# Graph attention layer on one core: one-hots in rows at a pitch of 130, own rows and tails joined from other places, marks and reciprocals in PSUM

## The chip, the core and the metric

The kernel runs on one core of a Trainium2 chip. The time is that of the device for one execution, in microseconds, and comparisons are made by medians of such executions. TensorE (PE; PEld are its weight loads), VectorE (DVE), ScalarE (ACT), GpSimd (POOL) and SyncE (SP) work side by side and meet at semaphores. GpSimd, SyncE and ScalarE also issue DMAs.

## What is computed

12500 nodes of 32 features and 400000 edges sorted by destination. Each node is normalised and projected by the matrix of its type; each edge gets a score from source, destination, edge type and attributes; the scores of a node's incoming edges go through a softmax, and the messages are summed with these weights.

```python
h = jnp.maximum(_layernorm(x, axis=-1), 0.0)
xl = jnp.einsum('ni,nio->no', h, hetero_w[node_type]) + hetero_b[node_type]
ete = _lrelu(edge_type_emb[edge_type]); eae = _lrelu(edge_attr @ edge_attr_w)
alpha = _lrelu(jnp.concatenate([xl[dst], xl[src], ete, eae], axis=-1) @ att_w)
alpha = jnp.exp(alpha - segment_max(alpha, dst)[dst])
alpha = alpha / (segment_sum(alpha, dst)[dst] + 1e-16)
msg = jnp.concatenate([xl[src], eae], axis=-1) @ lin_w * alpha
out = x + segment_sum(msg, dst)
```

## The kernel before

Each of 128 partitions has 3125 successive edges, worked on in 125 chunks of T = 25 edges a partition. Chunks go through U = 5 sets of buffers; a hardware loop runs 24 times over five chunks, and the last five stand behind it. A prologue builds a table of 12544 rows of 34 numbers (projected features and the two partial scores), stores it, splits the destinations into five digits, and sorts out constants.

In the loop a chunk needs three things. First, the table rows of its 25 sources. 22 of them come by an indirect DMA each, issued by GpSimd (`gather_chunk`, L494). GpSimd runs up to two chunks ahead (AHEAD = 2), and five turns within a chunk wait for what VectorE did for the chunk two earlier (picks, sums). The other 3 (TS) are computed: `select` (L697) multiplies one-hots of the source (7 groups of nodes, a 128 x 128 one-hot each) with the table in three bf16 parts, 21 matmuls of 462 columns; `take_product` (L1058) masks the result and `take_sum` (L1064) reduces it into `gath`. VectorE writes these one-hots in two pieces: tile 0 of a chunk in `select_first` (seven writes of 128, L1037), tiles 1 and 2 in `select_others` (seven of 256), into one set of buffers, so each piece waits for the matmuls that read the last one. Second, the destination scores: `dst_onehot` (L1084) writes a one-hot of 122 x 3200 from five loaded digits, `dst_scores` (L711) multiplies it with the scores, and `picks` (L1071) takes the maximum over 128 columns, in seven pieces. Third, messages from the edge attributes (L720, L742).

VectorE goes through these in a written order: picks 0 and 1, attribute activation, one-hots of tiles 1 and 2 of the next chunk, first product, pick 2, first sum, one-hots of tile 0 of the chunk after the next, pick 3, second product and sum, picks 4 to 6, `dst_onehot` of the next chunk, and only then the wait for the 22 gathers (L1122). Behind it come running maxima, exponentials (ScalarE) and two scans (L1167) that sum messages along the edges, and the third product. ScalarE copies the running sums into `rows` (L607) and stores them in `rows_dram`.

After the loop, places of each node's last edges are computed (`pos`). Then rows of nodes whose edges lie in two partitions are joined: SyncE loads each partition's last row (`tails`), VectorE and TensorE combine them (L1223 to L1238), GpSimd fetches each partition's own row (`own`, L509) and writes back the joined one (L512). The end gathers blocks of five rows for each of 98 nodes a partition (L534, 98 gathers), in eight buffers; VectorE marks the last row of a node (`is_node`, `is_last`), multiplies (L1305), reduces (L1307), divides and adds x, buffer by buffer, and SyncE stores.

## Time and profile before

| | us |
|---|---|
| median of 3 runs | 3876.05 (3875.31 to 3876.72) |
| the profiled execution | 3876.14 |
| its span, first to last instruction | 3874.1 |
| POOL busy | 2860.7 (74%) |
| PE busy | 2828.8 (73%) |
| DVE busy | 2479.5 (64%) |
| ACT busy | 877.0 (23%) |

The granted TensorE clock is 0.847 of full speed over the span. Busy shares are means over a prologue of some 180 us, the loop to about 3706 us, the joining to about 3728 us and the end. They don't tell who waits for whom; that is read from the idle time ahead of each line, which names the releaser ("issue" is time in which the engine waited for nothing that the profile shows), and from the timeline, where one sees which instructions of two engines overlap. A row of the timeline gives start, duration, engine, line, operation, what it writes and reads, and how often it is repeated.

### The profile page before, as it was taken

The numbers are of one execution on the slowest core, as the hardware profiler recorded it, in microseconds if no ns is written. First come the engines' busy times: TensorE is split into PE (matmuls) and PEld (weight loads), VectorE is DVE, ScalarE is ACT, GpSimd is POOL, SyncE is SP. The second block draws the span as 40 slices with busy tenths as digits, with TensorE's granted clock in tenths as the row PEclk, the third lists the DMA queues.
The fourth block names the chain that finished last, engine by engine and source line by source line (L and its number), as shares of the span: only waits on it lengthen the run. The fifth ranks groups of instructions, "written<-read, shape, count | busy, mean of one in ns | idle before, by whom it ended". The sixth has DMA issues, their size and how long they took to land.

```text
span 3874.1 us, 63674 instructions
## 1 busy us (share of the span) xinstructions
PE 2828.8 (73%) x19988; PEld 1707.6 (44%) x19988; DVE 2479.5 (64%) x7270; ACT 877.0 (23%) x2080; POOL 2860.7 (74%) x2868
## 2 busy tenths in 40 slices
PE   5388787777877777778787777877777778777710
PEld 4155444444444444444444444444444444444400
DVE  5677666666666666666666666666666666666625
ACT  2122222222222222222222222222222222222200
POOL 0777777777777777777777777777777777777757
PEclk9699888888888888888888888888888888888855
DMA  5433322322223222232222322322223223232122
GB/s 158 134 79 78 75 65 63 78 62 70 72 63 79 62 68 72 62 78 63 68 74 62 77 63 63 79 62 74 66 63 79 62 67 75 62 79 63 28 65 72
DMA packets 190147, 279.24 MB, mean 72 GB/s; under 512 B 76157, under 2 KB 145183, under 8 KB 189153
## 3 DMA queue, kind: packets, MB, share of 16 engines
q1 hardware_dynamic: 72864, 154.95, 13.3%
q0 software_dynamic: 92768, 56.87, 10.5%
q10 hardware_dynamic: 24288, 64.79, 4.5%
q8 instruction: 95, 1.56, 0.2%
q14 instruction: 132, 1.07, 0.1%
HBM read 204.11 MB, written 72.26 MB: 71 GB/s over the span
## 4 chain that ended last, share of the span: by engine, by line
POOL 35%; PE 26%; issue 16%; DVE 14%; DMA 6%; ACT 2%; POOLq 0%; DVEq 0%; SPq 0%; ACTq 0%
POOL gath L494 33%; PE ps_misc L697 18%; DMA gath<-table_dram,meta 4%; PE ps_msg L742 2%; PE ps_pick L711 2%; DVE h L1058 2%; DVE sums L1167 2%; DVE ps_msg L1122 2%; PE ps_attr L720 2%; DVE dscore L1071 2%; ACT keep L601 1%; POOL hib L534 1%; DVE ps_misc L1158 1%; PE ps_misc L664 1%; POOL hi_f L534 1%
## 5 line engine op out<-in xcount | busy, mean ns | idle before, releaser
L494 POOL DMA_INDIRECT gath<-table_dram,meta x2750 | 2750.3, 1000 | 944.6 <-issue 803.5
L697 PE MATMUL ps_misc<-parts,dst_f 128*128 128x462 bf16 x7875 | 1857.1, 398 | 431.3 <-DVE h L1058 423.2
L697 PEld LDWEIGHTS ps_misc<-parts,dst_f 128*128 128x128 bf16 x7875 | 817.4, 106 | 1350.7 <-DVE h L1058 432.1
L711 PE MATMUL ps_pick<-s_dst,onehot 122*128 122x128 bf16 x9375 | 652.4, 225 | 302.9 <-DVE sign_sums L1078 204.0
L711 PEld LDWEIGHTS ps_pick<-s_dst,onehot 122*128 122x128 bf16 x9375 | 578.9, 100 | 417.1 <-issue 244.9
L1058 DVE TENSOR_TENSOR h<-ps_misc,sel_mask 128x462 f32<-128x462 f32 x375 | 236.2, 630 | 738.6 <-PE ps_misc L697 735.5
L594 ACT ACTIVATE wts<-args 128x50 f32<-128x50 f32 x125 | 30.7, 245 | 2304.8 <-DVE args L1140 2304.8
L1071 DVE TENSOR_REDUCE dscore<-ps_pick 128x4 f32<-128x512 f32 x875 | 526.1, 625 | 8.1 <-PE ps_pick L711 4.3
L1122 DVE TENSOR_TENSOR ps_msg<-gath,ps_msg 128x495 f32<-128x495 f32 x250 | 135.7, 588 | 354.8 <-DMA gath<-table_dram,meta 354.8
L1037 DVE TENSOR_SCALAR dst_f<-dst_f,part_group 128x128 bf16<-128x128 f16 x1750 | 344.5, 276 | 1.1 <-DMA dst_f<-sel_code_dram 1.1
L607 ACT COPY rows<-sums 128x825 f32<-128x825 f32 x125 | 222.4, 1779 | 319.2 <-DVE sums L1167 319.2
L1167 DVE TENSOR_TENSOR_SCAN sums<-keep,ps_misc 128x416 f32<-128x416 f32 x250 | 261.8, 1047 | 27.6 <-ACT keep L601 21.4
L587 ACT ACTIVATE hi_f<-half,hic 128x128 bf16<-128x128 f32 x625 | 243.0, 389 | 61.4 <-ACT rows L607 60.5
L1064 DVE TENSOR_REDUCE gath<-h 128x33 f32<-128x462 f32 x375 | 236.8, 631 | 8.6
L589 ACT ACTIVATE hi_f<-half,loc 128x98 bf16<-128x98 f32 x625 | 225.7, 361 | 0.0
L742 PEld LDWEIGHTS ps_msg<-msg_w,node_buf 80*128 80x128 f32 x1250 | 188.8, 191 | 24.6
L742 PE MATMUL ps_msg<-msg_w,node_buf 80*128 80x165 f32 x1250 | 196.9, 305 | 0.0
L1158 DVE TENSOR_TENSOR ps_misc<-ps_msg,wts 128x240 f32<-128x240 f32 x500 | 159.0, 363 | 0.0
L720 PE MATMUL ps_attr<-attr,attr_w 80*80 80x320 f32 x500 | 158.1, 439 | 0.0
L1084 DVE TENSOR_SCALAR onehot<-hib,row_code 122x3200 bf16<-122x3200 bf16 x125 | 135.6, 1084 | 0.0
L601 ACT COPY keep<-wts 128x825 f32<-128x825 f32 x125 | 109.7, 878 | 0.0
L1097 DVE TENSOR_TENSOR node_buf<-node_buf,ps_attr 80x640 f32<-80x640 f32 x125 | 100.8, 806 | 0.0
(228 smaller groups left out, 1191.0 us busy)
## 6 DMA issues: line engine op xcount, KB each, us to landing
hib<-digit_dram SPq DMA_DIRECT2D x125, 612.5 KB
rows_dram<-rows ACTq DMA_DIRECT2D x125, 437.5 KB
gath<-table_dram,meta POOLq DMA_INDIRECT x2750
attr<-edge_attr_t_in SPq DMA_DIRECT2D x125, 200.0 KB
hib<-digit_dram SPq DMA_DIRECT2D x250, 50.0 KB
dst_f<-sel_code_dram SPq DMA_DIRECT2D x125, 96.0 KB
rows_dram<-gath ACTq DMA_DIRECT2D x1, 8575.0 KB, 45.7
hib<-digit_dram SPq DMA_DIRECT2D x250, 25.0 KB
```

The source lines that it names most:

```text
L494: nc.gpsimd.indirect_dma_start(gath[u][:, t, :], None, table_dram, bass.IndirectOffsetOnAxis(ap=meta_sb[u][:, t:t + 1], axis=0)).then_inc( ...
L587: nc.scalar.activation(sign_hi[:, t, :], half128[:], ACT.Sign, bias=hic[u][:, t:t + 1], scale=-1.0)
L589: last = nc.scalar.activation(sign_lo[:, t, :], half128[:, 0:NPP], ACT.Sign, bias=loc[u][:, t:t + 1], scale=-1.0)
L697: last = nc.tensor.matmul(ps_sel, sel_onehot[:, g, j * P:(j + 1) * P], parts[:, k, g, :], start=(g == 0 and k == 0), stop=(g == NG - 1 and ...
L711: last = nc.tensor.matmul(ps_pick[:, g % 2, j * LO:(j + 1) * LO], onehot[0:KD, t * P:(t + 1) * P], s_dst[0:KD, k, :], start=(k == 0), stop ...
L720: last = nc.tensor.matmul(ps_attr[0:G * F_EDGE, b, 0:TG * P // 2], attr_w[:], attr_sb[u][:, b * (TG * P // 2):(b + 1) * (TG * P // 2)], st ...
L742: last = nc.tensor.matmul(ps_msg[:, g // 3, g % 3 * G * VW:(g % 3 + 1) * G * VW], eae_flat[:, g * P:(g + 1) * P], msg_w[:], start=True, st ...
L1037: last = v.tensor_scalar(sel_onehot[:, g, tiles], code_sb[u][:, tiles], part_group[:, g:g + 1], None, ALU.is_equal)
L1058: v.tensor_tensor(sel_prod, ps_sel.rearrange("p (f n) -> p f n", n=GN), sel_mask[:, j:j + 1, :].broadcast_to([P, VW, GN]), ALU.mult).then_ ...
L1064: return step(v.tensor_reduce(gath[u][:, T - 1 - j, 0:VW], sel_prod, AX.X, ALU.add))
L1071: v.tensor_reduce(dscore[:, tiles], ps_pick[:, g % 2, 0:n * LO].rearrange("p (t m) -> p t m", m=LO), AX.X, ALU.max).then_inc(picked, 1)
L1167: last = v.tensor_tensor_scan(sums[:, f0:f1, :].rearrange("p f t -> p (f t)"), keep[:, f0:f1, :].rearrange("p f t -> p (f t)"), terms[:, 0 ...
```

## The change

1. The destination one-hot is `[P, T, ROW]` with ROW = 130: 25 rows of 128 written at a pitch of 130, from the same flat source of 3200. TensorE reads 128 of each row.
2. The selection one-hots get a set of buffers for each of the five chunks in flight, seven groups of 3 rows at the same pitch, in parts of `dst_f`, `hi_f`, `node_buf`, `h` and `hm`/`hmT`. `select_onehots` replaces both pieces: seven writes of 3 x 128 for the chunk after the next, behind pick 3, with no wait for matmuls. `select_masks` alone stays ahead of the first product.
3. At the joining, `tails` is copied on VectorE from `rows[U - 1]` in SBUF once ScalarE has written it; SyncE's DMA is gone. The own rows' gather no longer waits for the tails, as `head_idx_ready` is now raised in the prologue.
4. At the end `is_last` and the reciprocals lie in PSUM (banks of `ps_pick`) instead of SBUF.

```diff
+ROW = P + 2
+ROW_SET = TSM * ROW // 2
...
-        onehot = sb("onehot", [P, T * P], bf16)
+        onehot = sb("onehot", [P, T, ROW], bf16)
...
-        sel_onehot = dst_f[:, 0:NG * TSM * P // 2].bitcast(bf16).rearrange("p (g e) -> p g e", g=NG)
+        def onehot_rows(buf, at):
+
+            return [buf[:, at + g * ROW_SET:at + (g + 1) * ROW_SET].bitcast(bf16).rearrange("p (j e) -> p j e", e=ROW)
+                    for g in range(buf.shape[1] // ROW_SET) if at + (g + 1) * ROW_SET <= buf.shape[1]]
+        sel_onehot = [onehot_rows(dst_f, U * (TSM * P // 2))[0:NG], onehot_rows(hi_f, BPC * (P + NPP) // 2)[0:NG],
...
-        is_last = hm[1][:].rearrange("p a b -> p (a b)")[:, 0:NPP * BLOCK].rearrange("p (n j) -> p n j", j=BLOCK)
...
+        is_last = ps_pick[:, 0, 0:NPP * BLOCK].rearrange("p (n j) -> p n j", j=BLOCK)
+        per_sum = ps_pick[:, 1, 0:NPP]
...
-            with sp.If(flag < 1):
-                sp.dma_start(tails[:], rows_pm[:, EPP - 1, :]).then_inc(tails_in, 16)
-                sp.wait_ge(tails_in, 16)
...
-                pe.wait_ge(sel_onehot_ready if j else sel_first_ready, i * U + u + 1)
+                pe.wait_ge(sel_onehot_ready, i * U + u + 1)
...
-            def select_onehots(u, tiles, ready):
-
+            def select_onehots(i, u):
+
+                dve.wait_ge(code_in[u], (i + 1) * 16)
                 for g in range(NG):
-                    last = v.tensor_scalar(sel_onehot[:, g, tiles], code_sb[u][:, tiles], part_group[:, g:g + 1],
-                                           None, ALU.is_equal)
-                last.then_inc(ready, 1)
-
-            def select_first(i, u):
+                    last = v.tensor_scalar(sel_onehot[u][g][:, 0:TS[u], 0:P], code_sb[u][:, 0:TS[u] * P],
+                                           part_group[:, g:g + 1], None, ALU.is_equal)
+                last.then_inc(sel_onehot_ready, 1)
...
-                v.tensor_scalar(onehot[0:KD, :], hib_sb[u][0:KD, :], row_code[0:KD, :], None, ALU.is_equal).then_inc(
+                v.tensor_scalar(onehot[0:KD, :, 0:P], hib_sb[u][0:KD, :], row_code[0:KD, :], None, ALU.is_equal).then_inc(
...
-                    k_sel = select_others(*after)
+                    k_sel = select_masks(*after)
...
-                    if not isinstance(i, int) or c + 2 < CHUNKS:
-                        select_first(i if u < U - 2 else i + 1, (u + 2) % U)
                 picks(c, 3)
+                if not isinstance(i, int) or c + 2 < CHUNKS:
+                    select_onehots(i if u < U - 2 else i + 1, (u + 2) % U)
...
-                dve.wait_ge(tails_in, 16)
-                v.tensor_copy(mtail[:], tails[:, VW:VW + 1].broadcast_to([P, P])).then_inc(head_idx_ready, 1)
+                dve.wait_ge(rows_sums, count(CHUNKS))
+                v.tensor_copy(tails[:], rows[U - 1][:, T - 1, :])
+                v.tensor_copy(mtail[:], rows[U - 1][:, T - 1, VW:VW + 1].broadcast_to([P, P])).then_inc(tails_ready, 1)
...
-                finished(v.reciprocal(scale[:, 1, n], scale[:, 0, n]))
+                finished(v.reciprocal(per_sum[:, n], scale[:, 0, n]))
```

VectorE in a chunk of the loop, from the next chunk's first product on, before. `dst_f` on both sides of an arrow is the buffer that holds codes and one-hots.

```order
L1037 TENSOR_SCALAR dst_f<-dst_f,part_group 128x256 x7
L1052 ISA
L1052 TENSOR_TENSOR sel_mask<-sel_node,free 128x42
L817 REGISTER_ALU
L1057 REGISTER_ALU
L1058 TENSOR_TENSOR h<-ps_misc,sel_mask 128x462
L1068 REGISTER_ALU
L1071 TENSOR_REDUCE dscore<-ps_pick 128x4
L1064 TENSOR_REDUCE gath<-h 128x33
L1043 ISA
L1037 TENSOR_SCALAR dst_f<-dst_f,part_group 128x128 x7
L1068 REGISTER_ALU
```

And now, the same place (`node_buf` holds this chunk's set of one-hots):

```order
L1050 ISA
L1050 TENSOR_TENSOR sel_mask<-sel_node,free 128x42
L823 REGISTER_ALU
L1055 ISA
L1056 TENSOR_TENSOR h<-ps_misc,sel_mask 128x462
L1066 REGISTER_ALU
L1069 TENSOR_REDUCE dscore<-ps_pick 128x4
L1062 TENSOR_REDUCE gath<-h 128x33
L1066 REGISTER_ALU
L1069 TENSOR_REDUCE dscore<-ps_pick 128x4
L1042 ISA
L1044 TENSOR_SCALAR node_buf<-dst_f,part_group 128x3x128 x7
```

The writes ahead of the first product are gone, and the seven that stay write three rows each and have moved from ahead of pick 3 to behind it.

VectorE at the joining of rows, with the semaphores that an instruction waits for, before:

```order
L1220 COMPARE_AND_BRANCH
L1223 COPY mtail<-tails 128x128 [waits tails_in]
L1225 TENSOR_TENSOR mtail<-ps_misc,contrib 128x128 [waits mtail_mm]
L1226 TENSOR_SCALAR wtailT<-contrib 128x128 [waits join_step]
L1227 TENSOR_TENSOR mtail<-mtail,wtailT 128x128 [waits join_step]
L1228 TENSOR_REDUCE fix<-mtail 128x1 [waits join_step]
L1230 TENSOR_TENSOR fix<-fix,own 128x1 [waits own_in,join_step]
```

And now:

```order
L1218 COMPARE_AND_BRANCH
L1221 COPY tails<-rows 128x35 [waits rows_sums]
L1222 COPY mtail<-rows 128x128
L1224 TENSOR_TENSOR mtail<-ps_misc,contrib 128x128 [waits mtail_mm]
L1225 TENSOR_SCALAR wtailT<-contrib 128x128 [waits join_step]
L1226 TENSOR_TENSOR mtail<-mtail,wtailT 128x128 [waits join_step]
L1227 TENSOR_REDUCE fix<-mtail 128x1 [waits join_step]
L1229 TENSOR_TENSOR fix<-fix,own 128x1 [waits own_in,join_step]
```

The wait for the tails' DMA has become one for ScalarE's last copy; the copy into `tails` is added.

SyncE behind the loop, before:

```order
L364 TENSOR_LOAD unsorted_i [waits stored3,stored4,stored2,unsorted_ready,stored1,stored0]
L364 ISA x2
L444 DMA parts<-x_in 128x3136 [waits sel_mm]
L445 COMPARE_AND_BRANCH
L446 DMA tails<-rows_dram 128x35
L445 UNCONDITIONAL_BRANCH [waits tails_in]
```

And now:

```order
L374 TENSOR_LOAD unsorted_i [waits stored3,stored4,stored2,unsorted_ready,stored1,stored0]
L374 ISA x2
L454 DMA parts<-x_in 128x3136 [waits sel_mm]
L455 COMPARE_AND_BRANCH
L457 UNCONDITIONAL_BRANCH [waits node_rows_out]
```

The DMA of the tails and the wait for it are gone; what stands behind them follows at once.

## Rows read from the trace of the kernel before

**Rows 1.** The gathers' line L494: ns min/median/max; idle before it (us, times)

```profile
L494 POOL DMA_INDIRECT gath<-table_dram,meta x2750: 940/944/3912, 99.0 to 3697.4; - x197
  issue: 803.5, 2636
```

**Rows 2.** Windows, steady stretch: us; busy (x) of PE, PEld, DVE, ACT, POOL; clock

```profile
413.24:3672.30 3259.06, 2542.15 (x17899) 1519.84 (x17897) 2104.54 (x6378) 772.14 (x1846) 2494.89 (x2508) 0.86 0.27 68
```

**Rows 3.** Groups by shape, DVE, steady stretch: busy us, mean ns, idle before it

```profile
L1084 DVE TENSOR_SCALAR onehot<-hib,row_code 122x3200 bf16<-122x3200 bf16 x114 | 124.0, 1087 | 0.0
L1122 DVE TENSOR_TENSOR ps_msg<-gath,ps_msg 128x495 f32<-128x495 f32 x114 | 77.3, 678 | 342.3 <-DMA gath<-table_dram,meta 342.3
```

**Rows 4.** Waits of DVE, steady stretch: us in total, times, longest

```profile
DVE h L1058 <- PE ps_misc L697: 677.1, 209, 5.5
```

**Rows 5.** Timeline, one chunk: start us, us, what [idle before <-releaser]

```profile
1509.34 1.49 POOL L494 DMA_INDIRECT gath<-table_dram,meta  x1 [0.30 <-issue]
1509.34 1.50 DVE L1037 TENSOR_SCALAR dst_f<-dst_f,part_group 128x256 bf16<-128x256 f16 x7
1514.15 1.27 DVE L1037 TENSOR_SCALAR dst_f<-dst_f,part_group 128x128 bf16<-128x128 f16 x7
1514.87 0.94 POOL L494 DMA_INDIRECT gath<-table_dram,meta  x1 [0.30 <-issue]
1520.27 0.64 DVE L1058 TENSOR_TENSOR h<-ps_misc,sel_mask 128x462 f32<-128x462 f32 x1 [4.25 <-PE ps_misc L697]
1522.89 1.23 DVE L1084 TENSOR_SCALAR onehot<-hib,row_code 122x3200 bf16<-122x3200 bf16 x1
1523.61 1.32 POOL L494 DMA_INDIRECT gath<-table_dram,meta  x1 [0.30 <-issue]
```

**Rows 6.** Timeline of POOL, the 45th and the last gather

```profile
181.09 1.25 POOL L494 DMA_INDIRECT gath<-table_dram,meta  x1 [10.65 <-DVE dscore L1071]
...
3697.44 0.94 POOL L494 DMA_INDIRECT gath<-table_dram,meta  x1 [0.30 <-issue]
```

**Rows 7.** Timeline, the prologue's digits

```profile
108.08 1.79 DVE L943 CAST onehot<-node_buf 128x3125 bf16<-128x3125 int32 x1
108.47 3.35 POOL L494 DMA_INDIRECT gath<-table_dram,meta  x1 [0.30 <-issue]
```

**Rows 8.** Timeline, the end: VectorE's blocks and the gathers of rows

```profile
3754.30 3.42 DVE L1305 TENSOR_TENSOR node_buf<-node_buf,hm 128x3135 f32<-128x3135 f32 x1
3754.70 3.85 POOL L534 DMA_INDIRECT hi_f<-rows_dram,pos  x1 [0.30 <-issue]
3757.76 5.61 DVE L1307 TENSOR_REDUCE h<-node_buf 128x608 f32<-128x3040 f32 x1
3758.85 0.94 POOL L534 DMA_INDIRECT hi_f<-rows_dram,pos  x1 [0.30 <-issue]
...
3764.99 0.79 DVE L1313 TENSOR_TENSOR h<-h,parts 128x608 f32<-128x608 f32 x1
3765.10 1.49 POOL L534 DMA_INDIRECT hi_f<-rows_dram,pos  x1 [0.30 <-issue]
...
3854.33 1.86 POOL L534 DMA_INDIRECT hib<-rows_dram,pos  x1 [0.30 <-issue]
```

**Rows 9.** Chain that ended last, joining of rows: start us, us

```profile
3708.32 2.48 DMA rows_dram<-rows
3712.25 6.10 DMA tails<-rows_dram
3718.87 2.34 DMA own<-rows_dram,head_idx
```

**Rows 10.** Timeline of the DMA queue of SP, after the stores

```profile
3711.75 0.36 SPq L444 DMA_DIRECT2D parts<-x_in  x1
```

**Rows 11.** Timeline of DVE, before chunk 0

```profile
157.74 2.65 DVE L1037 TENSOR_SCALAR dst_f<-dst_f,part_group 128x128 bf16<-128x128 f16 x14 [1.08 <-DMA dst_f<-sel_code_dram]
...
177.70 1.23 DVE L1037 TENSOR_SCALAR dst_f<-dst_f,part_group 128x128 bf16<-128x128 f16 x7
```

More of the change, by code:

```diff
@@ L153, in gnn_kernel @@
         rows = [sb(f"rows{u}", [P, T, RW]) for u in range(U)]
-        onehot = sb("onehot", [P, T * P], bf16)
+        onehot = sb("onehot", [P, T, ROW], bf16)
         digit_i = node_buf[:, 0:EPP].bitcast(i32)
-        digit_b = [onehot[:, 0:EPP], *(b[:, 0:EPP] for b in hib_sb[1:])]
+        digit_b = [onehot[:].rearrange("p t e -> p (t e)")[:, 0:EPP], *(b[:, 0:EPP] for b in hib_sb[1:])]
         type_i = h[:].rearrange("p n f -> p (n f)")[:, 0:EPP].bitcast(i32)
@@ L175, in gnn_kernel @@
         sel_node = sb("sel_node", [P, SEL])
-        code_sb = [dst_f[:, (NG + u) * (TSM * P // 2):(NG + u + 1) * (TSM * P // 2)].bitcast(mybir.dt.float16)
-                   for u in range(U)]
-        sel_onehot = dst_f[:, 0:NG * TSM * P // 2].bitcast(bf16).rearrange("p (g e) -> p g e", g=NG)
+        code_sb = [dst_f[:, u * (TSM * P // 2):(u + 1) * (TSM * P // 2)].bitcast(mybir.dt.float16) for u in range(U)]
+        def onehot_rows(buf, at):
+            return [buf[:, at + g * ROW_SET:at + (g + 1) * ROW_SET].bitcast(bf16).rearrange("p (j e) -> p j e", e=ROW)
+                    for g in range(buf.shape[1] // ROW_SET) if at + (g + 1) * ROW_SET <= buf.shape[1]]
+        sel_onehot = [onehot_rows(dst_f, U * (TSM * P // 2))[0:NG], onehot_rows(hi_f, BPC * (P + NPP) // 2)[0:NG],
+                      onehot_rows(node_buf, 2 * TG * P)[0:NG],
+                      onehot_rows(h[:].rearrange("p n f -> p (n f)")[:, 0:T * NPP], 0)[0:NG],
+                      [row for b in (*hm, *(t[:].rearrange("p (a b) -> p a b", b=P) for t in hmT))
+                       for row in onehot_rows(b[:].rearrange("p a b -> p (a b)"), 0)][0:NG]]
         sel_mask = sb("sel_mask", [P, TSM, GN])
@@ L696, in select @@
                     for k in range(3):
-                        last = nc.tensor.matmul(ps_sel, sel_onehot[:, g, j * P:(j + 1) * P],
+                        last = nc.tensor.matmul(ps_sel, sel_onehot[u][g][:, j, 0:P],
                                                 parts[:, k, g, :], start=(g == 0 and k == 0),
@@ L1029, in _, with select_masks @@
             done(v.tensor_copy(head_idx[:, 0:1], head[:, 1:2]))
-            done(v.tensor_copy(head_idx[:, 1:2], head[:, 5:6]))
+            v.tensor_copy(head_idx[:, 1:2], head[:, 5:6]).then_inc(head_idx_ready, 1)
             done(v.tensor_scalar(contrib[:], free128[:], part[:, 0:1], None, ALU.is_lt))
             done(v.scalar_tensor_tensor(contrib[:], rlast[:], redge[:, 0:1], contrib[:], ALU.is_equal, ALU.mult))
-            def select_onehots(u, tiles, ready):
+            def select_onehots(i, u):
+                dve.wait_ge(code_in[u], (i + 1) * 16)
                 for g in range(NG):
-                    last = v.tensor_scalar(sel_onehot[:, g, tiles], code_sb[u][:, tiles], part_group[:, g:g + 1],
-                                           None, ALU.is_equal)
-                last.then_inc(ready, 1)
-            def select_first(i, u):
+                    last = v.tensor_scalar(sel_onehot[u][g][:, 0:TS[u], 0:P], code_sb[u][:, 0:TS[u] * P],
+                                           part_group[:, g:g + 1], None, ALU.is_equal)
+                last.then_inc(sel_onehot_ready, 1)
+            def select_masks(i, u):
                 c = i * U + u
-                dve.wait_ge(code_in[u], (i + 1) * 16)
-                if not isinstance(c, int) or c:
-                    dve.wait_ge(sel_mm, count(selected(i, u) - TS[u - 1] + 1))
-                select_onehots(u, slice(0, P), sel_first_ready)
-            def select_others(i, u):
-                c = i * U + u
-                dve.wait_ge(sel_mm, count(selected(i, u)))
-                select_onehots(u, slice(P, TS[u] * P), sel_onehot_ready)
                 return step(v.tensor_tensor(sel_mask[:], sel_node[:, ds(c * TSM, TSM)].unsqueeze(2).broadcast_to(
@@ L1178, in _ @@
             dve.wait_ge(table_out, 16)
-            select_first(0, 0)
-            need(select_others(0, 0), 0)
+            select_onehots(0, 0)
+            need(select_masks(0, 0), 0)
             dst_onehot(0, 0)
@@ L1184, in _ @@
                 need(take_sum(0, 0, j), 0)
-            select_first(0, 1)
+            select_onehots(0, 1)
             before = steps[0]
```

10 lines of the change are left out of this document (4 added, 6 removed).

## The prediction

> **What bounds the kernel now.** I read the gathers' line first. A gather is busy 0.944 us in the median and GpSimd then sits 803.5 / 2636 = 0.305 us before the next one although nothing holds it [rows 1], so an undisturbed gather costs 1.249 us. In the steady stretch, 413.24 to 3672.30 us, from one wait for gathers at L1122 to another, there are 2508 gathers in 3259.06 us [rows 2]: 22 for each of 114 chunks, 28.59 us a chunk, of which 22 x 1.249 = 27.48 is GpSimd's own pace. VectorE in the same stretch waits 342.3 us for gathers, 3.00 us a chunk [rows 3], so a chunk costs it 28.59 - 3.00 = 25.59 us with all its other waits. GpSimd is the bound, TensorE and VectorE follow.
>
> The missing 28.59 - 27.48 = 1.11 us a chunk is in the timeline [rows 5]. The gather at 1509.34 takes 1.49 instead of 0.94 us and ends with the seven one-hot writes of L1037; the one at 1523.61 takes 1.32 and ends 0.81 after L1084. The seven shorter writes at 1514.15 leave the gather at 1514.87 alone. The same is seen larger elsewhere: a gather of 3.35 us under the cast L943, which writes 3125 elements in 1.79 us [rows 7], and one of 3.85 us under L1305, a multiply with both operands in SBUF, while the longer reduce L1307 (5.61 us, one operand) leaves the gather at 3758.85 at 0.94 [rows 8]. So gathers wait for two kinds of VectorE work: single-source writes at more than the common pace (L943's 1750 elements a us, L1084's 3100, where L1305 does 917), and long operations with two SBUF operands. It is their kind that counts, not their length.
>
> **The loop.** The one-hots are the only long work of these kinds in the loop. The change leaves them in SBUF but writes them as 3 or 25 rows of 128 at a pitch of 130, from a source that stays one run. No row shows such a write. L943 and L1084, whose source and destination have one shape, hold gathers; L1307, with unlike shapes and one SBUF operand, does not [rows 5, 7, 8]. The new write has unlike shapes, so L1307 is the nearer row, and I take it that it no longer holds gathers up. The Trainium skill bears on exactly this: "VectorE: DVE Perf Modes", section "What auto-detection actually checks", says that a single-source operation uses both ports only if the outermost sizes of source and destination are both even or are equal, and "SBUF — State Buffer", section "Who interferes with whom", that without both ports and with one SBUF input it does not contend with GpSimd. 25 against 3200 and 3 against 384 are neither; by that rule the stalls go; without it the sum would stay at rival 3's.
>
> The price of the stalls: from the 45th gather (181.09, the first after GpSimd's one long wait for picks) to the last (3697.44) [rows 6] there are 2705 steps, and (3697.44 - 181.09) - 2705 x 1.249 = **137.8 us**. All of it comes back if VectorE keeps up. The bound on the other side is 0.
>
> Does it? L1084 takes 1.09 us [rows 3]. Its floor is to stay; its ceiling is L1305's pace, 3135 in 3.42 us [rows 8], that is 3200 in 3.5 us, or +2.4. Between them lies the pace of L943, 3125 in 1.79 us [rows 7], so 1.83 us; I take it, since it is the one pace between the two that the trace has for a single source: **+0.74 us a chunk**. This lies between the last pick and the wait for gathers, whose 3.00 us shrink first by 1.11 and then by 0.75. For the selection one-hots, seven writes of 256 take 1.50 and of 128 take 1.27 [rows 5], so 0.033 us per further 128 and 0.15 for each write alone. Seven of 384 are 1.75 us at that pace, 2.4 at half of it, 3.9 at a quarter. The 1.50 us ahead of the first product disappear, but VectorE then waits for TensorE's matmuls anyway; the new burst stands where 1.27 us stood, and the wait for the second product behind it is 4.25 us in this chunk [rows 5]; all waits for products are 677.1 us, 5.9 a chunk [rows 4]. Cover is there for 1.2 us more; without it they would cost 1.2 a chunk. So VectorE needs 25.59 + 0.74 = 26.3 us, some tenths more at most, against 27.5 of GpSimd: **the gathers remain the bound**, VectorE's wait for them falls to about 1.1 us a chunk. GpSimd's own waits in the loop are for picks and sums of two chunks earlier and stay met. TensorE no longer depends on one-hots of the chunk at hand, since all are made a chunk ahead; before, those of tiles 1 and 2 were written while it worked on tile 0 [rows 5], so that is 0.
>
> **The start.** GpSimd restarts at 181.09 only when chunk 0's first picks are done, so what comes before is on the path. TensorE could begin after seven writes of 128, half of the 2.65 us [rows 11]; now it waits for seven of 384: 2.4 - 1.3 = +1.1. Ahead of the first picks 1.23 us of writes [rows 11] become 2.4: +1.2. Together **+2.3 us** (+1.0 if the pace stays, +5 at L1305's pace). The longer L1084 there lies under the first product's matmuls.
>
> **The joining of rows.** Now the tails come by a DMA that starts after all stores and takes 6.10 us, and the own rows are fetched only after that, at 3718.87 [rows 9]. In the new order own rows wait for the stores alone: they land at 3708.32 + 2.48 = 3710.80, and SyncE, behind the same waits, issues at 3711.75 [rows 10]. So the gather starts at 3711.8 (bounds 3711.2 and 3712.8) in place of 3718.87: **-7.1 us** (-6 to -7.7). VectorE copies the tails from SBUF once its places are written, about 3710.5, and needs some 3 us to where it waits for own rows, which land at 3711.8 + 2.34 = 3714.1; they arrive last. The rest keeps its distances.
>
> **The end.** 98 gathers of rows are the path there too. L1305 holds one gather in each of seven blocks (the eighth comes after the last gather): 3.85 - 0.94 = 2.91 in the first [rows 8], then 2.47, 2.43, 1.31, 0.95, 0.91 and, in the last, 1.86 - 0.94 = 0.91 [rows 8]: 11.9 us. Marks in PSUM leave it one SBUF operand, as L1307 has, so the stalls go. The multiply by the reciprocals is freed likewise, but L1313 behind it still reads two SBUF operands and may hold what 0.55 [rows 8] and twice 0.3 us show; of these 1.2 us I take 0.4 as gone. **-12.3 us** (-11 to -13.1). The last block's chain after the last gather keeps its length: L1305 has no faster pace to lose.
>
> **Sum.** The profiled execution is 3876.14 us (span 3874.1 and 2.0 around it), 0.1 over the median: 3876.1 - 137.8 + 2.3 - 7.1 - 12.3 = 3721.2. Its own range is 3712 to 3732: the start's ends, the tail's ends, and up to 10 us of stalls under writes or short two-operand work that now falls elsewhere.
>
> **Rivals.**
> (1) Short stalls come anew. With the phase between VectorE and gathers moved, VectorE's short two-operand operations (0.16 to 0.3 us, six a chunk) fall on starts of gathers. They hardly do so now. At 0.2 us a chunk, 120 chunks: +24, 3745.
> (2) VectorE becomes the bound: the pitch costs the packed pace altogether and L1084 takes 3.5 us. 25.59 + 2.4 = 28.0 us a chunk exceeds 27.48; 114 x (28.0 - 28.59) = -67 in place of -127, start +5: 3876 - 67 + 5 - 19 = 3795. Against it: nothing in the elements' order within a row changes. The Trainium skill's rule for authors in "VectorE: DVE Perf Modes", section "Rules for kernel authors", wants dense, unit-step data for the highest pace and so speaks against this change; here L1084 would lose about a microsecond by it, which the wait for gathers covers.
> (3) The pitch changes nothing: same pace, same stalls, only the ends gain: 3876 - 7 - 12 + 1 = 3858.
> (4) **Slower.** The write goes slower and still holds gathers. Then the stall of L1084, 0.38 [rows 5], grows by its 0.75, and the stall of the selection writes, 0.55, by the 0.9 us that the burst is longer than 1.50. In place: +1.65 x 123 = +203, 3876 + 203 - 17 = 4062. It is slower from 17 / 123 = 0.14 us of added stall a chunk. For it: L943 holds gathers at just this pace [rows 7]. Against it: its source and destination have equal shape, and here they differ.
>
> **Chances.** The forecast 0.77, (1) 0.08, (2) 0.06, (3) 0.05, (4) 0.04. A measurement of this kernel can tell 0.2%, 8 us, from no change. (3) could end inside it if the longer burst holds more, for which I keep 0.02; so faster 0.94, same 0.02, slower 0.04. The range 3708 to 3762 holds the forecast and (1) with room above for a mixture with (2).
>
> **What would show it.** Gathers at a median of 0.94 with a mean near it in place of 1.00, and no gather of 1.3 to 1.5 under the one-hot writes; L1084's successor at about 1.8 us; VectorE's wait for gathers near 1.1 us a chunk and not 0; the own gather 1 us behind the stores' landing; no gather of 3.4 us at the end. If gathers are undisturbed and the time is still above 3760, VectorE or TensorE has become the bound, and GpSimd shows waits for picks. If L1084's successor shows 1.09 us or less, the pitch did nothing to the kind of the write, and the term of 137.8 falls.

## The result and the profile after

| | before | after |
|---|---|---|
| median of the runs | 3876.39 us (3875.31 to 3881.73, 4 runs) | 3724.95 us (3723.69 to 3725.99, 4 runs) |
| ratio to before | 1 | 0.9607, 95% interval 0.959 to 0.9623 |
| profiled execution | 3876.14 us, span 3874.1 | 3725.99 us, span 3723.9 |

The changed kernel is 151 us faster; 3721 was forecast. The lines have moved: the gathers' L494 is now L501, L1084 is L1082, L1037 is L1044, L1122 is L1120, the row gathers' L534 is L541 and L1305 is L1304.

First the gathers' line (the view of one line: shortest, median and longest in ns, first and last start; then the waits before it and who waited for it), which answers to [rows 1]:

```profile
L501 POOL DMA_INDIRECT gath<-table_dram,meta x2750: 938/944/3347, 98.9 to 3562.3; - x197
  issue: 818.0, 2684
...
  DVE ps_msg L1120: 126.1, 85
```

The same gathers in the page's list of groups (busy us, mean ns), of before and then of after:

```profile
L494 POOL DMA_INDIRECT gath<-table_dram,meta x2750 | 2750.3, 1000 | 944.6 <-issue 803.5
```
```profile
L501 POOL DMA_INDIRECT gath<-table_dram,meta x2750 | 2610.9, 949 | 948.8 <-issue 818.0
```

The median gather is 0.944 us in both; the mean fell from 1000 to 949 ns, and 2750 x 0.051 = 140 us is nearly the whole gain. From the first gather to the last it is 3598.4 us before [rows 1] and 3463.4 now, 135.0 less.

The writes and VectorE's wait for gathers, by shape, in a steady stretch of 115 chunks (413.24 to 3540 us); they answer to [rows 3] and [rows 5]:

```profile
L1082 DVE TENSOR_SCALAR onehot<-hib,row_code 122x3200 bf16<-122x3200 bf16 x115 | 215.2, 1871 | 0.0
L1120 DVE TENSOR_TENSOR ps_msg<-gath,ps_msg 128x495 f32<-128x495 f32 x115 | 77.8, 677 | 116.6 <-DMA gath<-table_dram,meta 116.5
L1044 DVE TENSOR_SCALAR hi_f<-dst_f,part_group 128x384 bf16<-128x384 f16 x161 | 53.5, 405 | 0.0
```

The long write takes 1.87 us where it took 1.09, and VectorE's wait for gathers is 116.6 / 115 = 1.01 us a chunk where it was 3.00. The timeline of one chunk shows the gather at 1502.48 whole under the long write and the one at 1493.74 whole under the burst of seven, both 0.94 us:

```profile
1493.61 2.32 DVE L1044 TENSOR_SCALAR hi_f<-dst_f,part_group 128x384 bf16<-128x384 f16 x7
1493.74 0.94 POOL L501 DMA_INDIRECT gath<-table_dram,meta  x1 [0.30 <-issue]
...
1501.74 1.87 DVE L1082 TENSOR_SCALAR onehot<-hib,row_code 122x3200 bf16<-122x3200 bf16 x1
1502.48 0.94 POOL L501 DMA_INDIRECT gath<-table_dram,meta  x1 [0.30 <-issue]
```

The ends of the loop, and the end of the kernel, in the timeline; they answer to [rows 6] and [rows 8]:

```profile
182.50 0.94 POOL L501 DMA_INDIRECT gath<-table_dram,meta  x1 [13.03 <-DVE dscore L1069]
...
3562.32 0.94 POOL L501 DMA_INDIRECT gath<-table_dram,meta  x1 [0.30 <-issue]
...
3616.42 3.42 DVE L1304 TENSOR_TENSOR node_buf<-node_buf,ps_pick 128x3135 f32<-128x3135 f32 x1
3616.81 0.95 POOL L541 DMA_INDIRECT hi_f<-rows_dram,pos  x1 [0.30 <-issue]
```

From the 45th gather to the last there are (3562.32 - 182.50) - 2705 x 1.249 = 1.3 us of stall, where there were 137.8. Summed up one by one, the gathers over 1.0 us in the trace before account for it: what they take beyond the median is 137.7 us, 53.9 under the destination's write and 83.6 under the bursts of 256. Now no gather behind the 45th takes over 1.0 us. At the end L1304 takes as long as L1305 did (3.42 us), but the gather under it takes 0.95 where it took 3.85.

The chain of work that ended last, in the joining of rows (start, us, what), answers to [rows 9]:

```profile
3573.09 2.49 DMA rows_dram<-rows
...
3575.78 0.51 POOLq L374
...
3576.91 0.04 POOLq L514
3576.95 3.26 issue
3580.21 3.09 DMA own<-rows_dram,head_idx
```

### The profile page after: what moved, and what is told of

Its sections match the earlier page's. It is cut to its first block, busy times and chain, and to the rows that moved or that the text cites. A ratio compares the mean times of both kernels' runs of the same rounds, so it can differ in the third digit from the quotient of the medians.

```text
span 3723.9 us, 62625 instructions
## 1 busy us (share of the span) xinstructions
PE 2800.8 (75%) x19988; PEld 1690.7 (45%) x19988; DVE 2541.3 (68%) x6396; ACT 876.6 (24%) x2080; POOL 2709.0 (73%) x2868
## 3 DMA queue, kind: packets, MB, share of 16 engines
q0 software_dynamic: 92768, 56.87, 10.8%
## 4 chain that ended last, share of the span: by engine, by line
POOL 40%; PE 23%; issue 18%; DVE 13%; DMA 4%; ACT 2%; POOLq 1%; DVEq 0%; SPq 0%; ACTq 0%
POOL gath L501 38%; PE ps_misc L704 16%; DMA gath<-table_dram,meta 2%; PE ps_msg L749 2%; PE ps_pick L718 2%; DVE h L1056 2%; DVE sums L1165 2%; DVE ps_msg L1120 2%; PE ps_attr L727 2%; DVE dscore L1069 1%; DVE onehot L1082 1%; ACT keep L608 1%; POOL hib L541 1%; DVE ps_misc L1156 1%; PE ps_misc L671 1%
## 5 line engine op out<-in xcount | busy, mean ns | idle before, releaser
L501 POOL DMA_INDIRECT gath<-table_dram,meta x2750 | 2610.9, 949 | 948.8 <-issue 818.0
L704 PE MATMUL ps_misc<-parts,dst_f 128*128 128x462 bf16 x1575 | 370.1, 397 | 97.0 <-DVE h L1056 89.3
L704 PE MATMUL ps_misc<-parts,node_buf 128*128 128x462 bf16 x1575 | 372.7, 399 | 89.0 <-DVE h L1056 89.0
L704 PE MATMUL ps_misc<-parts,h 128*128 128x462 bf16 x1575 | 370.6, 397 | 89.6 <-DVE h L1056 89.6
L704 PE MATMUL ps_misc<-parts,hm 128*128 128x462 bf16 x1575 | 367.5, 395 | 91.5 <-DVE h L1056 91.5
L704 PE MATMUL ps_misc<-parts,hi_f 128*128 128x462 bf16 x1575 | 372.2, 398 | 81.5 <-DVE h L1056 78.9
L704 PEld LDWEIGHTS ps_misc<-parts,dst_f 128*128 128x128 bf16 x1575 | 163.3, 106 | 280.3 <-DVE h L1056 91.8
L704 PEld LDWEIGHTS ps_misc<-parts,node_buf 128*128 128x128 bf16 x1575 | 164.0, 106 | 272.4 <-DVE h L1056 89.2
L704 PEld LDWEIGHTS ps_misc<-parts,h 128*128 128x128 bf16 x1575 | 163.4, 106 | 271.6 <-DVE h L1056 90.1
L704 PEld LDWEIGHTS ps_misc<-parts,hm 128*128 128x128 bf16 x1575 | 162.5, 105 | 271.2 <-DVE h L1056 92.1
L704 PEld LDWEIGHTS ps_misc<-parts,hi_f 128*128 128x128 bf16 x1575 | 163.9, 106 | 265.2 <-DVE h L1056 79.8
L1082 DVE TENSOR_SCALAR onehot<-hib,row_code 122x3200 bf16<-122x3200 bf16 x125 | 233.9, 1871 | 0.0
```

The lines of the kernel that those rows point to most:

```text
L501: nc.gpsimd.indirect_dma_start(gath[u][:, t, :], None, table_dram, bass.IndirectOffsetOnAxis(ap=meta_sb[u][:, t:t + 1], axis=0)).then_inc( ...
L704: last = nc.tensor.matmul(ps_sel, sel_onehot[u][g][:, j, 0:P], parts[:, k, g, :], start=(g == 0 and k == 0), stop=(g == NG - 1 and k == 2))
L1082: v.tensor_scalar(onehot[0:KD, :, 0:P], hib_sb[u][0:KD, :], row_code[0:KD, :], None, ALU.is_equal).then_inc(onehot_ready, 1)
```

## The experiments

Twelve kernels were run, four on each of three chips. On two of the chips something else is the bound, as "Eight kernels on chips where TensorE is late" shows; on the third the kernel before takes 3880.38 us (3875.86 to 3886.82, 13 runs), as on the chip of the result. The four kernels of that chip come first.

### Four lightened kernels: TensorE relieved

TensorE was relieved, in both kernels alike, so that it cannot be the bound: of the three bf16 parts of the table and of the scores only one is multiplied.

```diff
-                    for k in range(3):
+                    for k in range(1):
                         last = nc.tensor.matmul(ps_sel, sel_onehot[u][g][:, j, 0:P],
...
-                    for k in range(3):
+                    for k in range(1):
                         last = nc.tensor.matmul(ps_pick[:, g % 2, j * LO:(j + 1) * LO],
...
```

The kernel before, lightened:

> The kernel before, of which TensorE leaves out two of the three parts of the picked numbers (42 of 63 selection products and 50 of 75 destination products of a chunk); its output is therefore only roughly the reference's. TensorE then has 92 products a chunk less, and the gathers are the bound on this chip too. Theory (VectorE's writes hold the gathers that stand under them): as in the trace of before, some 110 gathers under the destination one-hots and some 120 under the selection writes take 45 to 55 and 75 to 90 us more, the loop from the 45th gather to the last stalls 130 to 145 us over its pace of 1.249 us, and the time is 130 to 150 us over that of the lightened changed kernel. Rival (the gain came from the order of work on VectorE and TensorE, not from gathers that were held): with TensorE relieved the two come within 20 us of each other.

The changed kernel, lightened:

> The changed kernel with the same two thirds of the products left out (its output too is only roughly the reference's). Theory: no gather is held from the 45th on, mean 0.944 to 0.95 us, and the loop stalls less than 3 us over its pace, as in the trace of the changed kernel; 130 to 150 us under the lightened kernel before. Rival: within 20 us of it.

The changed kernel, lightened, with the destination one-hot in two writes and the marks in SBUF:

```diff
-                v.tensor_scalar(onehot[0:KD, :, 0:P], hib_sb[u][0:KD, :], row_code[0:KD, :], None, ALU.is_equal).then_inc(
-                    onehot_ready, 1)
+                v.tensor_scalar(onehot[0:KD, 0:T - 1, 0:P], hib_sb[u][0:KD, 0:(T - 1) * P], row_code[0:KD, :], None,
+                                ALU.is_equal)
+                v.tensor_scalar(onehot[0:KD, T - 1, 0:P], hib_sb[u][0:KD, (T - 1) * P:], row_code[0:KD, :], None,
+                                ALU.is_equal).then_inc(onehot_ready, 1)
...
-        is_last = ps_pick[:, 0, 0:NPP * BLOCK].rearrange("p (n j) -> p n j", j=BLOCK)
-        per_sum = ps_pick[:, 1, 0:NPP]
+        is_last = hm[1][:].rearrange("p a b -> p (a b)")[:, 0:NPP * BLOCK].rearrange("p (n j) -> p n j", j=BLOCK)
+        per_sum = scale[:, 1, :]
```

> The lightened changed kernel with two parts undone in different stages. In the loop, the destination one-hot is written as 24 rows and one row of 128 at the pitch of 130 (number of rows even); at the end, the marks and the reciprocals stand in SBUF again. Theory (the number of rows decides): the long write takes 1.01 us instead of 1.87 and holds the gathers under it, 40 to 60 us more in the loop; rival (the pitch or the new place keeps the gathers free): 0 in the loop. At the end the 98 row gathers stall 12 to 13 us more (13.15 against 0.85 in the two traces); rival (the stall is that of the rows' own data): 0. Together by the theory 52 to 73 us over the lightened changed kernel.

The changed kernel, lightened, with the selection one-hots in one run of 384 and the old joining:

```diff
-                    last = v.tensor_scalar(sel_onehot[u][g][:, 0:TS[u], 0:P], code_sb[u][:, 0:TS[u] * P],
+                    last = v.tensor_scalar(sel_onehot[u][g][:, 0:TS[u] * P], code_sb[u][:, 0:TS[u] * P],
...
+            with sp.If(flag < 1):
+                sp.dma_start(tails[:], rows_pm[:, EPP - 1, :]).then_inc(tails_in, 16)
+                sp.wait_ge(tails_in, 16)
...
```

> The lightened changed kernel with two other parts undone in different stages. In the loop the selection one-hots are written without gaps, 384 elements in a row; at the joining the tails are fetched from DRAM again. Theory (three rows at a pitch keep the gathers free): the burst takes 1.69 us instead of 2.33, and the gathers under it, 1 to 1.3 in a chunk, are held until it ends, 0.5 to 1 us each: 60 to 100 us more in the loop. Rival (one burst instead of two, or the new places, freed them): less than 15 us. At the joining 2 to 7 us more from the last message to the first row gather (28.6 against 25.9 in the two traces, 7.1 by the prediction).

Measured, with the ratio to the kernel before and its interval:

| lightened | median us | ratio |
|---|---|---|
| before | 3878.86 (3872.89 to 3879.71, 10 runs) | 0.999 (0.998 to 1.000) |
| changed | 3719.70 (3715.04 to 3721.28, 4 runs) | 0.9583 (0.9567 to 0.9599) |
| changed, 24 + 1 rows, marks in SBUF | 3784.20 (3779.17 to 3784.99, 4 runs) | 0.9749 (0.9733 to 0.9765) |
| changed, runs of 384, old joining | 3728.32 (3727.59 to 3731.03, 4 runs) | 0.9607 (0.9591 to 0.9623) |

The gathers' line of the four, in this order (as above: shortest, median, longest, first and last start):

```profile
L494 POOL DMA_INDIRECT gath<-table_dram,meta x2750: 940/945/3346, 99.2 to 3699.1; - x197
```
```profile
L501 POOL DMA_INDIRECT gath<-table_dram,meta x2750: 940/944/3346, 100.8 to 3551.7; - x197
```
```profile
L501 POOL DMA_INDIRECT gath<-table_dram,meta x2750: 938/944/3912, 99.9 to 3602.4; - x197
```
```profile
L505 POOL DMA_INDIRECT gath<-table_dram,meta x2750: 940/945/3911, 99.9 to 3561.5; - x197
```

**Held gathers are the gain.** TensorE's busy time fell from 2828.8 to 1704.9 us, and the kernel before takes the same time as ever. Between lightened before and lightened changed the loop, first gather to last, differs by 3599.9 - 3450.9 = 149.0 us. From the 45th gather on, 247 gathers of the lightened kernel before take over 1.0 us, which is 143.5 us beyond the median in all, and none of the lightened changed one. The rival, that the gain came from the order of the other engines' work, is out.

**Destination one-hots: the number of rows decides.** With the pitch of 130 kept and only the 25th row split off, the loop is 3502.5 us long, 51.6 more. The page's group shows the long write back at the common pace:

```profile
L1082 DVE TENSOR_SCALAR onehot<-hib,row_code 122x3072 bf16<-122x3072 bf16 x125 | 128.8, 1030 | 0.0
```

and its timeline a gather held until the write is over (both in one chunk):

```profile
1504.03 1.16 POOL L501 DMA_INDIRECT gath<-table_dram,meta  x1 [0.30 <-DVE dscore L1069]
1504.07 1.01 DVE L1082 TENSOR_SCALAR onehot<-hib,row_code 122x3072 bf16<-122x3072 bf16 x1
```

From the 45th gather on, 124 gathers that overlap this write took over 1.0 us, 52 us beyond the median in all, which is what the loop is longer; in the lightened changed kernel 273 overlap the write of 25 rows and none took over 0.96. The 25 rows were what the change needed, not the pitch alone: at a pitch of 130, 24 rows take 1.03 us and hold gathers, 25 rows take 1.87 and do not. Other numbers of rows were not tried. The Trainium skill states this condition in "VectorE: DVE Perf Modes", section "What auto-detection actually checks" (outermost sizes both even, or equal); these two runs agree with it on both sides.

**Selection one-hots: it was mostly not the pitch.** Written in one run of 384 they cost the loop 3461.6 - 3450.9 = 10.7 us, not 60 to 100. The group of one of the five buffers, and the two gathers that start under one burst:

```profile
L1049 DVE TENSOR_SCALAR dst_f<-dst_f,part_group 128x384 bf16<-128x384 f16 x175 | 44.5, 323 | 1.2 <-DMA dst_f<-sel_code_dram 1.2
```
```profile
1512.79 1.77 DVE L1049 TENSOR_SCALAR node_buf<-dst_f,part_group 128x384 bf16<-128x384 f16 x7
1512.84 0.95 POOL L505 DMA_INDIRECT gath<-table_dram,meta  x1 [0.30 <-issue]
1514.09 1.05 POOL L505 DMA_INDIRECT gath<-table_dram,meta  x1 [0.30 <-issue]
```

Of the gathers under these bursts 80 took over 1.0 us, and the longest took 1.05: 8 us in all. In the lightened kernel before it is another picture:

```profile
1505.02 1.55 POOL L494 DMA_INDIRECT gath<-table_dram,meta  x1 [0.30 <-issue]
1505.09 1.51 DVE L1037 TENSOR_SCALAR dst_f<-dst_f,part_group 128x256 bf16<-128x256 f16 x7
...
1508.47 1.22 DVE L1037 TENSOR_SCALAR dst_f<-dst_f,part_group 128x128 bf16<-128x128 f16 x7
1509.38 0.97 POOL L494 DMA_INDIRECT gath<-table_dram,meta  x1 [0.30 <-issue]
```

Counted from the 45th gather on, 123 of the 127 gathers that overlap a burst of 256 were held, 112 of them to within 0.06 us of the burst's end, 82 us in all; the other four were nearly done when the burst began. Of 240 at the bursts of 128 none took over 1.0 us. So in this kernel seven writes of 256 in a row hold a gather for the whole burst, seven of 128 do not hold it, and seven of 384 hold it by 0.1 us at most. It is not where the gather stands when the burst begins: with 256, the 112 gathers that were then at most 0.6 us old all took 1.5 us or more, with 384 the 108 of that age took 0.95 at most.

The pitch therefore adds only the last 11 us at the selection one-hots. The rest of that gain came with what else the change does there, and these things were not separated: one burst of 384 in place of 128 and 256, its place behind pick 3, and other buffers, in which the groups start 780 bytes apart and no longer 768. That the writes left dst_f is not the reason: in the runs of 384 the one-hots that still lie there show the same 0.1 us as those that moved. Why 256 differs from 384 at the same pace stays open. "SBUF — State Buffer" of the Trainium skill, section "Who interferes with whom", has the second comer fully blocked while such a write runs; the bursts of 256 and the 24-row write agree, the bursts of 384 and 128 do not show it.

**Marks in PSUM.** With the marks in SBUF the row gathers span 3765.5 - 3631.0 = 134.5 us, without 3701.4 - 3580.2 = 121.2: 13.3 us (the reciprocals went back with them). The timeline of the third kernel has the 3.85 us of [rows 8] back:

```profile
3656.94 3.42 DVE L1306 TENSOR_TENSOR node_buf<-node_buf,hm 128x3135 f32<-128x3135 f32 x1
3657.33 3.85 POOL L541 DMA_INDIRECT hi_f<-rows_dram,pos  x1 [0.30 <-issue]
```

**The joining.** From the last gather to the first row gather it is 3592.8 - 3561.5 = 31.3 us in the old order and 3580.2 - 3551.7 = 28.5 in the new: 2.8 us. The same comes out of the two unlightened traces: 3728.4 - 3697.4 = 31.0 and 3590.5 - 3562.3 = 28.2. The 2 to 7 expected are met at their lower end, and the 7.1 of the prediction are not.

For the third kernel the terms add up: 51.6 in the loop, 13.3 at the end, -0.9 at the first gather and +0.1 at the joining are 64.1, and the medians differ by 64.5. For the fourth they are 10.7, -0.9 and 2.8, 12.6 us, as the two traced executions differ; the medians differ by 8.6, since the traced execution of the lightened changed kernel is 4.7 us below its median.

### Eight kernels on chips where TensorE is late

The single parts were first undone one by one in the full kernel, with the same edits as above (the first has the destination one-hot in one run of 3200).

> The changed kernel with the destination one-hot written flat again (one run of 3200, no pitch); the selection one-hots keep their rows. My theory, the shape of source against destination decides whether a write holds gathers: the write goes back from 1.87 to 1.09 us, gathers that start under it take 1.3 us and more again, about 0.4 us of stall a chunk, in all +50 us against the changed kernel's 3725, so 3775 (3760 to 3790). Rival, the separate buffers or the new places of the writes freed the gathers: no stall returns, 3725 or a little less since VectorE has 0.8 us a chunk less to do.

> The changed kernel with the selection one-hots written flat (seven writes of 384 in one run each) into the same separate buffers and at the same new place behind pick 3; the destination one-hot keeps its rows. Shape theory: a write takes 0.25 instead of 0.33 us, the burst about 1.75 us, and it holds one or two gathers a chunk: +0.5 to +1.0 us a chunk, 3725 + 60 to 120 = 3785 to 3845. Rival, the place of the burst mattered and not its kind (the old burst ahead of pick 3 left its gather alone, the one ahead of the first product did not): near 3725.

> The changed kernel, pitch of 130 everywhere, but the destination one-hot is written by two instructions: 24 rows of 128, then one row. Only the number of rows in a write is changed. Shape theory (even row count and even source fall back into the fast kind): the write of 24 rows takes 1.0 us instead of 1.87, its stalls return, about +0.4 us a chunk, 3765 to 3785. Rival, the pitch itself (where the rows lie) frees the gathers: the write takes 1.8 us, no stalls, 3725 to 3727.

> The one-hot of the destination digits keeps its pitch of 130, but is written as 24 rows of 128 and then one row of 128, 3072 and 128 elements, in two instructions. Theory (the number of rows decides, not the pitch): the long write falls back from 1.87 us to 1.0 us and holds gathers under it again; before, the nine gathers under the two writes of a chunk pair cost 0.4 us more each, 47 us over the loop, so about +40 us, 3755 to 3785. Rival (the pitch itself keeps the gathers free, or the length of the write does): the kernel stays at the time of the changed kernel, 3725, with the long write at 1.87 us.

> The seven selection one-hots of a chunk are written without a gap between rows (384 elements in a row) instead of three rows of 128 at a pitch of 130. Theory (rows at a pitch keep the gathers free): each write takes 0.30 to 0.32 us instead of 0.40, the burst 1.7 us instead of 2.33 and some gathers under it are held again: before, 116 gathers under these writes took 74 us more; now they stand in one burst per chunk, one or two gathers of 1.3 to 1.6 us under each, so +40 to +75 us, 3765 to 3800. Rival: the selection writes never held the gathers once they are in one burst, and the kernel stays at 3725 or gains the 0.6 us a chunk of VectorE.

| kernel | us | ratio to before on the same chip |
|---|---|---|
| chip A: before | 4908.28 (7 runs) | |
| destination in one run | 4935.36 | 1.0051 (1.0034 to 1.0068) |
| selection in runs of 384 | 4938.93 | 1.0058 (1.0041 to 1.0074) |
| 24 + 1 rows | 4937.54 | 1.0056 (1.0039 to 1.0072) |
| early branch (below) | 4939.06 | 1.0056 (1.0039 to 1.0073) |
| chip B: before | 5008.24 (7 runs) | |
| 24 + 1 rows | 4970.51 | 0.9925 (0.9908 to 0.9942) |
| selection in runs of 384 | 4974.22 | 0.9927 (0.9910 to 0.9943) |
| early branch, late x (below) | 4970.03 | 0.9923 (0.9906 to 0.9939) |
| the same, three chunks ahead | 4985.61 | 0.9955 (0.9939 to 0.9972) |

None of the expected differences can be seen here. (The changed kernel as it stands was not run on these two chips; the kernels are compared with each other.) The reason is in the page's groups of the 24 + 1 rows kernel on chip B:

```profile
L501 POOL DMA_INDIRECT gath<-table_dram,meta x2750 | 2620.3, 953 | 2143.5 <-DVE dscore L1069 1295.2
L1069 DVE TENSOR_REDUCE dscore<-ps_pick 128x4 f32<-128x512 f32 x875 | 539.9, 630 | 1239.8 <-remote 1172.4
L704 PE MATMUL ps_misc<-parts,h 128*128 128x462 bf16 x1575 | 434.9, 432 | 169.6 <-issue 165.0
```

against the last two of these lines in the changed kernel on the chip of the result:

```profile
L1069 DVE TENSOR_REDUCE dscore<-ps_pick 128x4 f32<-128x512 f32 x875 | 526.8, 626 | 8.4 <-PE ps_pick L718 4.8
L704 PE MATMUL ps_misc<-parts,h 128*128 128x462 bf16 x1575 | 370.6, 397 | 89.6 <-DVE h L1056 89.6
```

TensorE's products come with gaps for which the trace shows no wait (issue), VectorE stands idle 1239.8 us before its picks where it was 8.4 (for most of it the profile names no releaser, "remote"), and GpSimd waits 1295 us for VectorE. The gathers are then started by VectorE's picks, always at the same point of its work: in the first kernel 123 of the 124 that start under the long write start 0.87 us after it, when it has 0.17 to go, and take 0.99.

```profile
2016.82 1.04 DVE L1082 TENSOR_SCALAR onehot<-hib,row_code 122x3200 bf16<-122x3200 bf16 x1
2017.69 0.99 POOL L501 DMA_INDIRECT gath<-table_dram,meta  x1 [5.71 <-DVE dscore L1069]
```

What these runs do give are durations that don't depend on the bound: the long write in one run takes 1.044 us and in 25 rows 1.870, the same kernel otherwise, so the slower write is the 25 rows' price. What makes TensorE late on these chips, and why the changed forms lose 0.6% on one and gain 0.8% on the other, is open; the four kernels of a chip lie within 0.1% of each other save the last one.

### The joining: the branch and the load of x

In the result's trace GpSimd reads the flag (0.51 us in the chain above, 1.3 with what is around it) and passes a branch after the stores have landed, and then nothing is shown for 3.26 us until its gather starts at 3580.21, while SyncE's load of x, issued at 3576.53, is under way. Two edits take these out, first the branch alone (GpSimd reads the flag and branches, and waits for the stores only in the arm that it took), then both:

```diff
-            for u in range(U):
-                pool.wait_ge(stored[u], 16 * ITERS + 1)
...
+                for u in range(U):
+                    pool.wait_ge(stored[u], 16 * ITERS + 1)
```
```diff
-            sp.dma_start(x_sb, x).then_inc(x_in, 16)
+            with sp.If(flag < 1):
+                sp.wait_ge(own_in, 16)
+                sp.dma_start(x_sb, x).then_inc(x_in, 16)
...
```

> The changed kernel; GpSimd reads the flag for sorted input and takes the branch before it waits for the last stores instead of after, so the own rows' gather is the first thing behind that wait. In the changed kernel this gather came 4.6 us after the stores had landed: 1.3 us of reading and branching, and 3.3 us in which nothing is shown. Theory A, these 3.3 us are spent once behind the branch (the instructions there are not at hand yet): both pass while GpSimd waits anyway, the gather starts within 0.5 us of the landing, -4.3 us, 3720.6. Theory B, they belong to this gather itself, the first from another tensor: only 1.3 us go, 3723.6. Theory C, stores land later than SyncE's issue suggests: no change.

> Of the changed kernel two things at the joining move: GpSimd takes the branch on the flag before it waits for the stores, not behind that wait, and SyncE loads x only when the own rows have landed. Theory: GpSimd spends 3.3 us behind the branch with no wait shown (3576.9 to 3580.2) and 0.8 us of it stay once it is passed early, and the own rows land 2.4 us after their gather instead of 3.2, as before the change: 4 to 5 us less from the last message to the first row gather (25.9 to 21 to 22), 3720 to 3721. Rival 1: the 3.3 us belong to the gather itself (its descriptors), and only 0.8 us go, 3724. Rival 2: x, loaded later, ends up late for what the end needs, and the time is 3727 or more.

The chain of the first (chip A), in the joining:

```profile
4785.94 2.48 DMA rows_dram<-rows
...
4788.58 0.77 issue
4789.34 6.01 DMA own<-rows_dram,head_idx
```

and of the second (chip B):

```profile
4817.20 2.48 DMA rows_dram<-rows
4819.84 0.77 issue
4820.61 2.44 DMA own<-rows_dram,head_idx
```

The stretch with nothing shown goes from 3.26 us (3.40 and 3.37 in the 24 + 1 rows kernels of the two chips) to 0.77: it belongs to the branch, not to the gather, which settles it against the rival that the gather itself takes it. But with the branch alone the gather and the load of x are issued 0.03 us apart, and own rows take 6.01 us to land; from the stores' DMA to the first row gather it is 16.65 us, where the 24 + 1 rows kernel of chip A has 17.76.

With x behind them own rows take 2.44 us. Then x is loaded beside the write of the joined rows, which takes 2.92 us where it takes 2.20 in the 24 + 1 rows kernel of chip B: what the later load gains at own rows it loses there. From the stores' DMA to the first row gather the kernel with both edits has 4830.99 - 4817.20 = 13.79 us, that 24 + 1 rows kernel 4828.75 - 4810.61 = 18.14, 4.35 us less. Of these 0.57 are not the edits': the last stores took 3.05 us to land in the one trace and 2.48 in the other. The 3.8 that are left, a little under the expected 4 to 5, all come from the flag and the branch: the own gather starts 0.93 us after the stores land, where it is 4.74. On the clock 4 us are not to be told there.

The last kernel lets GpSimd run three chunks ahead besides:

```diff
-AHEAD = 2
+AHEAD = 3
```

> As the kernel with the early branch and the late load of x, and GpSimd also runs three chunks ahead with its gathers instead of two. Theory: the gathers of the third chunk no longer wait 13 us at the start for the picks (the wait before 182.5 us), and VectorE with 26.2 us a chunk against 27.3 of GpSimd keeps up, so the loop starts earlier and the total is 13 + 4.6 us less, about 3707. Rival: the stall is only moved to where the next buffer comes free (VectorE works its first eight chunks at 25.6 us each and the lead is used up later), and the time is that of the early branch alone, about 3720.

GpSimd's long wait for picks at the start does not go, it moves: with two chunks ahead it stands before the 45th gather and lasts 20.61 us (the kernel with both edits), with three before the 67th, at 213.55 us, and lasts 18.57. Gathers are then ahead of the other kernel's, the 67th by 12.7 us and the last by 13.0 (4761.41 against 4774.36), but the last stores are issued 10.8 us later (4827.95 against 4817.20): this chip is bound elsewhere, and the time is 15.6 us over that of the kernel without it. Whether three chunks ahead gain where gathers are the bound was not tried, so neither theory is decided, and 3707 stays an estimate.

## Why the prediction was right, and where it was not

| step | forecast us | measured us |
|---|---|---|
| loop, stall of the gathers | -137.8 | -136.5 |
| start | +2.3 | +1.4 |
| joining | -7.1 | -2.8 |
| end, row gathers | -12.3 | -12.3 |
| whole, profiled execution | 3721.2 | 3725.99 |

- **The bound.** GpSimd's pace of 1.249 us a gather was the floor, and VectorE kept under it: it waits 1.01 us a chunk for gathers (forecast 1.1), and the lightened pair shows that TensorE has no part in it. One reading of the rows was off and touches no term: L1084's pace is 3200 elements in 1.087 us [rows 3], some 2940 a us and not 3100.
- **The price of the writes.** 1.83 us for the long one, taken from L943's pace, was measured as 1.871. Seven of 384 take 2.33 us (forecast 2.4, the half-pace value).
- **Why the stalls go.** For the destination one-hots the step was right, and the 24 rows show it. For the selection one-hots the sum was right and the reason wrong: the prediction ascribed all stalls to the kind of write, and took the pitch to be what removes them. In fact the timeline it quoted had the exception in it: the burst of seven 128-wide writes left its gather alone [rows 5]. The prediction noted it and still put the stalls down to the kind of write; the row says that not every write of this kind holds gathers, so that replacing 128 and 256 by one burst of 384 needed a term of its own. Of the 83.6 us held at the selection writes before, some 11 hang on the pitch. That the others went too, without the reason given for them, is luck.
- **The start** was sized a microsecond too high. It covers two bursts of 2.33 us in place of 2.65 / 2 + 1.23: +1.0 and +1.1 make 2.1, and the first gather after the wait is 1.4 later. The first burst begins at 157.28 us, where it began at 157.74 [rows 11], which is 0.5 of the difference.
- **The joining is the mis-sized term**, 4.3 us. The forecast put the own gather 1 us after the stores land, by SyncE's issue at 3711.75 [rows 10]. It started 4.6 after (3573.09 + 2.49 = 3575.58 to 3580.21): 1.3 us for the flag and 3.3 behind the branch. In the trace before, GpSimd did the same work while tails were still on their way, so no wait pointed to it: own gathers started at 3718.87, 0.5 us after the tails [rows 9], which hid it. And own rows took 3.09 us to land, not the 2.34 of [rows 9], because x is now loaded beside them; alone they take 2.44, and issued at one moment with x 6.01.
- **The end** came to 12.3 us as forecast, and with the marks and the reciprocals alone undone it is 13.3.
- **Rivals.** New short stalls (1) did not come: two steps of 2705 in the loop are over 1.27 us. VectorE as the bound (2), no effect (3) and a held slower write (4) did not come either; but with 24 rows instead of 25, (3) would have been true for the destination one-hots.

## What to carry to other kernels

When GpSimd's gathers set the pace, look for VectorE writes that stand over gathers longer than the median, and sort them by shape before ascribing them to a rule: here 3200 in one run and 24 rows of 128 hold gathers, 25 rows do not, and of the short ones only those of 256 do for the whole burst. A write that takes 0.8 us more can make a kernel faster if VectorE has that time, and the number of rows is then a tool (25 and 3 here, not 24). When a wait is removed, look at what its engine did meanwhile, sequencer instructions included: a flag read and a branch that cost nothing before came to 4.6 us.

## What was not expected of the hardware

- Seven one-hot writes of 256 elements hold a gather until they are over, 1.5 us and more, seven of 384, no slower per element, by 0.1, and seven of 128 not at all.
- After a branch GpSimd shows nothing for 3.26 us before its next DMA. With the branch ahead of the wait for the stores, 0.77 us are left between that wait and the DMA.
- A gather of the own rows lands in 2.4 us alone, in 3.1 when the load of x was issued 3.7 us before, in 6.0 when they are issued together. The write of the joined rows takes 2.9 us in place of 2.2 with that load beside it.
- The same kernel before takes 3.88 ms in the result and beside the four lightened kernels, and 4.91 and 5.01 ms on two other chips, where TensorE's work has gaps without a shown wait. With TensorE at 1704.9 us of work instead of 2828.8 its granted clock fell from 0.85 to 0.64, and the time stayed the same.
